# Half of the rotary sum moves from GpSimd to VectorE: the queries' 256 columns, behind the maximum

## The chip, the cores and the metric

The kernel runs on one core of one Trainium2 chip. The metric is the device time of one execution, in microseconds. A core has five engines that run their own instruction streams and meet at semaphores: TensorE (PE; PEld is its weight load), VectorE (DVE), ScalarE (ACT), GpSimd (POOL) and SyncE (SP, which issues the DMAs here).

## What is computed

The program is a decoder block on 32 sequences of 128 tokens and 128 channels: a causal self-attention, a cross-attention, and then a stack of six layers with windowed attention and a gated MLP. The change lies in the windowed attention of the six layers:

```
def attn_layer(x, Wqkv, qs, ksc, Wo):
    q, k, v = jnp.split(x @ Wqkv, 3, -1)            # 16 heads of 64
    q = l2norm(q) * qs
    k = l2norm(k) * ksc
    q = q * cos * scale + rotate_half(q) * sin * scale
    k = k * cos * inv   + rotate_half(k) * sin * inv
    out = local_attention(q, k, v)                  # window 32, looks one window back
    return out @ Wo
...
for i in range(6):
    x = attn_layer(shift_tokens(x), ...) + x
    x = ffn_layer(shift_tokens(x), ...) + x
```

The sum in the two lines of `q` and `k` is the rotary sum that this case is about.

## The kernel before

Everything stays in SBUF. Each of the six layers has 32 sequences times 4 groups of 4 heads, so 128 groups. One step of a software pipeline takes in one new group and works on several older ones at the same time: at step j the group j is projected, rotated and squared, the group j-3 is transposed (`win_heads`), the group j-5 gets its scores and its maximum, j-6 its exponentials and the scaling by the row sum, j-7 the transposition of the probabilities and the sum over the values, j-8 the output projection. Eight steps (two sequences) are the body of a hardware loop; steps 0 to 4 of a layer are written out separately and lie between the MLP of the layer before (`first` and `finish_into`). 30 of the 768 groups are in such opening steps, 738 in the main part. The MLP of the layer follows, partly woven into the drain.

There is no scheduler: each engine's order is written by hand, in its own block of the program, and waits are semaphore counts. In the main part VectorE does in each step, in this order: `win_cos` (L1487, projection times cosine table, 128x512 from PSUM), `win_sin` (L1495, projection with swapped halves times sine table), the reciprocal of the row sums (L1527), `win_scale` (L1537, probabilities), `win_max` (L1519), `win_norms` (L1502, sums of squares), `win_clamp` (L1512, small), and in some steps `win_tok` (L1463), `win_split` (L1469) and `win_add` (L1544), each of 128x128 and once in four steps. The latter three always stand in an odd step.

GpSimd does in each step `win_rotate` (L1206: `rotated = by_cos + by_sin`, 512 columns, 256 of the queries and 256 of the keys, all in SBUF), in each odd step `win_rnorm` (L1214: the power -1/2 of the 16 norms of two groups), and in each even step `win_unit` (L1226: two products of `rotated` by the norm's inverse). `win_unit` hands the group to TensorE's transposition (L691) by the semaphore `c_unit`. `win_cos` waits on the semaphore of `win_rotate` of two groups before (`c_rotated`), since the buffers `by_cos` and `by_sin` are two deep; `rotated` is four deep and comes free when TensorE has transposed the group (`c_heads`).

ScalarE does in each step the four exponentials of a group (L1052), the copy of the transposed probabilities (L1069), the squares (L1043), the copy of values and sums (L1063) and the copy of the transposed queries and keys (L1034). TensorE has in each step the projection (L698), the transposed probabilities (L757), band and scores (L730, L741), the value sum (L771), the transposition of heads (L691) and the output projection (L793).

Of the kernel before, what the change touches and what calls it, by code (L numbers as in the profile page):

```python
# [17 lines left out]
ALU = mybir.AluOpType  # L18
# [8 lines left out]
GROUPS = NB * NG  # L27
# [18 lines left out]
STEPS = 2 * NG  # L46
# [90 lines left out]
def has(index):  # L137

    return not isinstance(index, int) or index >= 0


def in_range(it, j, lag, n):

    return not isinstance(it, int) or 0 <= it * n[1] + j - lag < n[0]


def build(nc, x_in, ctx_in, a_w, a_m, b_wq, b_bq, b_wk, b_bk, b_wv, b_bv, b_wo, b_bo, wqkv, q_scale, k_scale,
          wo, ln_g, ln_b, w1, b1, w2, b2, const_d, out):
    with ExitStack() as stack:
# [3 lines left out]
        def ring(name, n, shape, dt=F32):  # L153
            return [sb(f"{name}{i}", shape, dt) for i in range(n)]
# [54 lines left out]
        by_cos = ring("by_cos", 2, [P, 2, HG, DH])  # L209
        by_sin = ring("by_sin", 2, [P, 2, HG, DH])  # L210
# [3 lines left out]
        rotated = ring("rotated", 4, [P, 2, HG, DH])  # L214
# [53 lines left out]
        def sem(name):  # L268
            return stack.enter_context(nc.semaphore(name))
# [90 lines left out]
        c_sin = sem("c_sin_done")  # L360
# [2 lines left out]
        c_nrm2 = sem("c_norm2")  # L363
        c_nrm2g = sem("c_norm2_guarded")
        c_rn = sem("c_rnorm")
        c_rot = sem("c_rotated")
        c_unit = sem("c_unit")
        c_heads = sem("c_heads")
        c_qk = sem("c_qk_ready")
# [71 lines left out]
        def here(it, j, lag):  # L441
            return in_range(it, j, lag, (GROUPS, STEPS))
# [720 lines left out]
        def _(pool):  # L1163
# [35 lines left out]
            def win_rotate(layer, it, j):  # L1199
                if here(it, j, 0):  # L1200
                    g = layer * GROUPS + it * STEPS + j
                    pool.wait_ge(c_sin, g + 1)
                    if has(it * STEPS + j - 4):

                        pool.wait_ge(c_heads, g - 3)
                    nc.gpsimd.tensor_tensor(rotated[j % 4][:, :, :, :], by_cos[j % 2][:, :, :, :], by_sin[j % 2][:, :, :, :], ALU.add).then_inc(c_rot, 1)  # L1206

            def win_rnorm(layer, it, j):
                if j % 2 == 1 and here(it, j, 1):
# [7 lines left out]
            def win_unit(layer, it, j):  # L1217
                if j % 2 == 0 and here(it, j, 2):
                    g = layer * GROUPS + it * STEPS + j - 2
                    u = layer * UNITS + it * (STEPS // 2) + j // 2 - 1  # L1220
                    slot = (j // 2 - 1) % 2
                    pool.wait_ge(c_rn, u + 1)
                    pool.wait_ge(c_rot, g + 2)
                    for i in range(2):
                        at = rotated[(j - 2) % 4 + i][:, :, :, :].rearrange("t a h d -> t (a h) d")
                        nc.gpsimd.tensor_tensor(at, at, rnorm[slot][:, i, :].unsqueeze(2).to_broadcast([P, 2 * HG, DH]), ALU.mult).then_inc(c_unit, 1)  # L1226

            def win_step(layer, it, j):
                win_rotate(layer, it, j)
                win_rnorm(layer, it, j)  # L1230
                win_unit(layer, it, j)
# [97 lines left out]
        def _(dve):  # L1329
# [141 lines left out]
            def win_tok_next(layer, it, j):  # L1471
                if j % NG == 1 and here(it, j, -2 * NG + 1):
                    win_tok(layer, it * 2 + j // NG + 2, j // NG)

            def win_split_next(layer, it, j):
                if j % NG == 3 and here(it, j, -2 * NG + 3):
                    win_split(layer, it * 2 + j // NG + 2, j // NG)

            def win_cos(layer, it, j):
                if here(it, j, 0):  # L1480
                    g = layer * GROUPS + it * STEPS + j
                    if has(it * STEPS + j - 2):

                        dve.wait_ge(c_rot, g - 1)
                    dve.wait_ge(c_proj, g + 1)
                    got = proj_ps[:, :].rearrange("t (a h d) -> t a h d", a=2, h=HG)
                    nc.vector.tensor_tensor(by_cos[j % 2][:, :, :, :], got, table(rot_cos, layer).unsqueeze(2).to_broadcast([P, 2, HG, DH]), ALU.mult).then_inc(c_cos, 1)  # L1487

            def win_sin(layer, it, j):
                if here(it, j, 0):  # L1490
                    if isinstance(it, int) and it == 0 and j == 0:
                        dve.wait_ge(c_sines, 2 * (layer + 1))
                    got = proj_ps[:, :].rearrange("t (n s d) -> t n s d", s=2, d=HALF)[:, :, ::-1, :]
                    rows = lambda b: b[:, :, :, :].rearrange("t a h (s d) -> t (a h) s d", s=2)
                    nc.vector.tensor_tensor(rows(by_sin[j % 2]), got, rows(sin_now), ALU.mult).then_inc(c_sin, 1)  # L1495

            def win_norms(layer, it, j):
                if here(it, j, 0):
                    g = layer * GROUPS + it * STEPS + j
                    dve.wait_ge(c_sq, g + 1)  # L1500
                    pair = norm2[j % 2]
                    nc.vector.tensor_reduce(pair[:, :, 0:1], squares[:, :, :], AX_X, ALU.add).then_inc(c_nrm2, 1)  # L1502

            def win_clamp(layer, it, j):
                if here(it, j, 0):
                    g = layer * GROUPS + it * STEPS + j
                    pair = norm2[j % 2]
                    dve.wait_ge(c_nrm2, g + 1)
                    if j % 2 == 0 and has(it * STEPS + j - 4):

                        dve.wait_ge(c_rn, layer * UNITS + it * (STEPS // 2) + j // 2 - 1)
                    nc.vector.tensor_reduce(norm2g[j // 2 % 2][:, j % 2, :].unsqueeze(2), pair[:, :, :], AX_X, ALU.max).then_inc(c_nrm2g, 1)  # L1512

            def win_max(layer, it, j):
                if here(it, j, WIN.top):
                    m = layer * GROUPS + it * STEPS + j - WIN.top
                    slot = (j - WIN.top) % 2
                    dve.wait_ge(c_scores, m + 1)
                    nc.vector.tensor_reduce(top[slot][:, :].rearrange("q (e i) -> q e i", e=2), win_ps[slot].rearrange("q e (i k) -> q e i k", i=2),  # L1519
                                            AX_X, ALU.max, negate=True).then_inc(c_top, 1)  # L1520

            def win_recip(layer, it, j):
                if here(it, j, WIN.scale):
                    m = layer * GROUPS + it * STEPS + j - WIN.scale
                    jl = (j - WIN.scale) % STEPS
                    dve.wait_ge(c_exp, m + 1)
                    nc.vector.reciprocal(rsum[jl % 2][:, :], psum_raw[jl % 2][:, :]).then_inc(c_rsum, 1)  # L1527

            def win_scale(layer, it, j):
                if here(it, j, WIN.scale):  # L1530
                    m = layer * GROUPS + it * STEPS + j - WIN.scale
                    jl = (j - WIN.scale) % STEPS
                    dve.wait_ge(c_rsum, m + 1)
                    if has(it * STEPS + j - WIN.scale - 2):

                        dve.wait_ge(c_pturn, m - 1)
                    nc.vector.tensor_tensor(prob[jl % 2][:, :, :].rearrange("q (e i) k -> q e i k", e=2), win_ps[jl % 2].rearrange("q e (i k) -> q e i k", i=2),  # L1537
                                            rsum[jl % 2][:, :].rearrange("q (e i) -> q e i", e=2).unsqueeze(3).to_broadcast([P, 2, 2, P]), ALU.mult).then_inc(c_scaled, 1)

            def win_add(layer, it, j):  # L1540
                if j % NG == 3 and here(it, j, WIN.out + NG - 1):
                    b = it * 2 + (j - WIN.out - NG + 1) // NG
                    dve.wait_ge(c_wo, layer * NB + b + 1)
                    nc.vector.tensor_tensor(seq(y, b), seq(y, b), acc_ps[:, 0:P], ALU.add).then_inc(c_yadd, 1)  # L1544

            def win_step(layer, it, j):
                win_cos(layer, it, j)
                win_sin(layer, it, j)
                win_recip(layer, it, j)
                win_scale(layer, it, j)  # L1550
                win_max(layer, it, j)
                win_norms(layer, it, j)
                win_clamp(layer, it, j)
                win_tok_next(layer, it, j)
                win_split_next(layer, it, j)
                win_add(layer, it, j)
# [93 lines left out]
            def win_rotations(layer, j):  # L1650
                win_cos(layer, 0, j)
                win_sin(layer, 0, j)

            def win_squares(layer, j):
                win_norms(layer, 0, j)
                win_clamp(layer, 0, j)
# [124 lines left out]
```

## Time and profile before

| | |
|---|---|
| device time, median of 3 runs | 4208.51 us (4206.87 to 4213.31) |
| the profiled execution | 4210.7 us, of which its span is 4208.9 us |
| TensorE busy | 3918.9 us (93%) |
| VectorE busy | 3703.7 us (88%) |
| ScalarE busy | 3550.0 us (84%) |
| GpSimd busy | 3379.4 us (80%) |

A line of the groups view names the line of the program, the engine, the operation, output and inputs, the count, then the busy time with the mean of one instruction, then the time for which the engine idled just before these instructions and what ended that idle time. Instructions of one engine overlap a little: the recorded duration of one is longer than the distance to the start of the next. A timeline row gives start and duration in microseconds. In the views over a part of the span, a window is given in microseconds from the start of the span.

### The profile page before, as it was taken

The page shows a single profiled execution, that of the slowest core. Times are in us where ns is not written, and L with a number is a line of the kernel's source. Part 1 is how long each engine was busy: PE and PEld are TensorE (multiplying, and loading weights), DVE is VectorE, ACT ScalarE, POOL GpSimd, SP SyncE. Part 2 cuts the span into 40 slices and gives each one's busy share as a digit, 9 for nine tenths or more (in the row PEclk, how much of TensorE's full clock was granted, in tenths as well). Part 3 has the DMA queues.
Part 4 walks back from the last instruction along what each step waited for, and adds up shares of the span by engine and source line. Part 5 has one row for each costly group of instructions (what it writes and reads, how often), then busy time and mean ns, then how long its engine had stood idle before and what let it go on. Part 6 is the DMA issues. An engine that isn't in the chain of part 4 may idle for free.

```text
span 4208.9 us, 137255 instructions
## 1 busy us (share of the span) xinstructions
PE 3918.9 (93%) x49504; PEld 3102.0 (74%) x49504; DVE 3703.7 (88%) x8896; ACT 3550.0 (84%) x11595; POOL 3379.4 (80%) x2461
## 2 busy tenths in 40 slices
PE   7998885999999999989999999999899999999998
PEld 5666664777777777777777777777777777777776
DVE  7998887999988999979999889999799998899996
ACT  6888995999977999959999779999599997699995
POOL 4554446999978999969999789999599997799993
PEclk9999997999999999999999999999999999999999
DMA  3000000000000000010000000000100000000001
GB/s 84 0 0 1 0 0 16 3 2 0 0 21 22 5 0 0 1 41 4 2 0 0 15 28 5 0 0 1 41 4 2 0 0 13 15 5 0 0 1 36
DMA packets 81122, 38.89 MB, mean 9 GB/s; under 512 B 60084, under 2 KB 73266, under 8 KB 80946
## 3 DMA queue, kind: packets, MB, share of 16 engines
q1 hardware_dynamic: 80946, 36.56, 3.3%
q8 instruction: 108, 1.77, 0.2%
q14 instruction: 68, 0.56, 0.0%
HBM read 21.92 MB, written 2.10 MB: 6 GB/s over the span
## 4 chain that ended last, share of the span: by engine, by line
ACT 42%; PE 33%; DVE 13%; issue 10%; POOL 2%; ACTq 1%; SPq 0%; DMA 0%; DVEq 0%; POOLq 0%
ACT pair L1052 20%; PE bank L771 12%; ACT prob_t L1069 7%; ACT vout L1063 6%; ACT qk_t L1034 5%; PE bank L691 5%; PE pair L848 4%; PE bank L698 3%; DVE top L1443 3%; PE bank L793 2%; DVE qk_parts L1418 2%; PE bank L864 2%; PE bank L672 1%; DVE by_sin L1411 1%; ACT prob L977 1%
## 5 line engine op out<-in xcount | busy, mean ns | idle before, releaser
L1214 POOL TENSOR_TENSOR rnorm<-norm2g,neg_half 128x16 f32<-128x16 f32 x384 | 1115.3, 2905 | 181.7 <-DVE norm2g L1512 172.4
L1052 ACT ACTIVATE pair<-pair,top 128x128 f32<-128x128 f32 x3072 | 1055.8, 345 | 34.9 <-DVE top L1519 24.2
L1206 POOL TENSOR_TENSOR rotated<-by_cos,by_sin 128x512 f32<-128x512 f32 x768 | 985.8, 1284 | 51.0 <-DVE by_sin L1495 44.4
L1226 POOL TENSOR_TENSOR rotated<-rotated,rnorm 128x512 f32<-128x512 f32 x768 | 785.3, 1043 | 0.5
L698 PE MATMUL bank<-wqkv_high,xt_high 128*128 128x512 f32 (+1 forms) x1536 | 649.5, 423 | 15.9 <-ACT squares L1043 14.5
L1052 ACT ACTIVATION_READ_ACCUMULATOR pair<-pair,top 128x1 f32 x3072 | 652.3, 212 | 0.0
L1487 DVE TENSOR_TENSOR by_cos<-bank,rot_cos 128x512 f32<-128x512 f32 x768 | 529.9, 690 | 108.2 <-PE bank L698 91.5
L1063 ACT ACTIVATE vout<-bank 128x512 f32<-128x512 f32 (+1 forms) x810 | 466.0, 575 | 150.5 <-PE bank L771 145.1
L771 PE MATMUL bank<-prob_t,vout 128*32 128x128 f32 x12288 | 495.2, 279 | 94.0 <-ACT prob_t L1069 56.8
L1537 DVE TENSOR_TENSOR prob<-pair,rsum 128x512 f32<-128x512 f32 x768 | 530.9, 691 | 40.0
L1043 ACT ACTIVATE squares<-bank 128x512 f32<-128x512 f32 x768 | 458.8, 597 | 109.7 <-DVE by_sin L1495 92.0
L1502 DVE TENSOR_REDUCE norm<-squares 128x8 f32<-128x512 f32 x768 | 519.3, 676 | 11.3 <-ACT squares L1043 9.9
L1519 DVE TENSOR_REDUCE top<-pair 128x4 f32<-128x512 f32 x768 | 522.4, 680 | 0.7
L1495 DVE TENSOR_TENSOR by_sin<-bank,sin_now 128x512 f32<-128x512 f32 x768 | 522.4, 680 | 0.0
L698 PE MATMUL bank<-wqkv_low,xt_high 128*128 128x512 f32 (+1 forms) x1536 | 520.6, 339 | 0.0
L698 PE MATMUL bank<-wqkv_high,xt_low 128*128 128x512 f32 (+1 forms) x1536 | 520.1, 339 | 0.0
L1196 POOL TENSOR_TENSOR kz_parts<-qk_parts,cst 128x512 fp32r<-128x512 f32 x256 | 266.2, 1040 | 307.4 <-DVE qk_parts L1418 307.4
L691 PE MATMUL bank<-cst,rotated 128*128 128x128 f32 x3072 | 504.3, 287 | 2.7 <-POOL rotated L1226 2.5
L1069 ACT ACTIVATE prob_t<-bank 128x512 f32<-128x512 f32 x768 | 474.3, 618 | 4.8 <-PE bank L757 4.8
L793 PE MATMUL bank<-wo_sb,vout 128*128 128x128 f32 x3072 | 472.8, 276 | 2.0 <-ACT vout L1063 2.0
L771 PEld LDWEIGHTS bank<-prob_t,vout 128*32 128x32 f32 x12288 | 289.8, 109 | 239.6 <-ACT prob_t L1069 196.5
L757 PE MATMUL bank<-cst,prob 128*128 128x128 f32 x3072 | 461.8, 273 | 1.4 <-ACT qk_t L1034 1.4
(142 smaller groups left out, 8451.6 us busy)
## 6 DMA issues: line engine op xcount, KB each, us to landing
wqkv_sb<-in_L_ffn_Wqkv_dram SPq DMA_DIRECT2D x36, 256.0 KB, 4.0
ctx_all<-y SPq DMA_DIRECT2D x48, 128.0 KB
ctx_all<-y SPq DMA_DIRECT2D x48, 127.0 KB
wo_sb<-in_L_ffn_Wo_dram SPq DMA_DIRECT2D x48, 64.0 KB, 2.0
out_dram<-y SPq DMA_DIRECT2D x8, 256.0 KB, 3.5
w_sb<-in_L_ffn_W_dram SPq DMA_DIRECT2D x6, 341.0 KB, 3.0
w_sb<-in_L_ffn_W_dram SPq DMA_DIRECT2D x12, 64.0 KB
cst<-in_constants_dram SPq DMA_DIRECT2D x1, 582.0 KB, 3.9
```

The source lines that it names most:

```text
L691: last = nc.tensor.transpose(turned_ps(it)[:, k * P:(k + 1) * P], flat[:, k * P:(k + 1) * P], ident)
L698: last = nc.tensor.matmul(dst, a[slot][:, :], w[:, which, cols], start=(n == 0), stop=(n == 2))
L771: last = nc.tensor.matmul(value_ps[PAD * h:PAD * (h + 1), half * P:(half + 1) * P], vout[jl][:, at:at + PAD], prob_t[jl % 2][:, h % 2 * 2 ...
L793: last = nc.tensor.matmul(acc_ps[:, 0:P], vout[(j - 1) % STEPS][:, half * P:(half + 1) * P], wo_sb[:, k * P:(k + 1) * P], start=(k == 0), ...
L1052: last = nc.scalar.activation(at, at, ACT.Exp, bias=top[jl % 2][:, h:h + 1], accum_out=psum_raw[jl % 2][:, h:h + 1])
L1063: nc.scalar.activation(vout[j][:, cols], value_ps[:, cols], ACT.Copy).then_inc(c_vout, 1)
L1069: nc.scalar.activation(prob_t[(j - WIN.probs) % 2][:, :, :].rearrange("k h q -> k (h q)"), turn_c_ps[:, :], ACT.Copy).then_inc(c_pt, 1)
L1206: nc.gpsimd.tensor_tensor(rotated[j % 4][:, :, :, :], by_cos[j % 2][:, :, :, :], by_sin[j % 2][:, :, :, :], ALU.add).then_inc(c_rot, 1)
L1214: nc.gpsimd.tensor_tensor(rnorm[slot][:, :, :].rearrange("t g n -> t (g n)"), norm2g[slot][:, :, :].rearrange("t g n -> t (g n)"), neg_hal ...
L1226: nc.gpsimd.tensor_tensor(at, at, rnorm[slot][:, i, :].unsqueeze(2).to_broadcast([P, 2 * HG, DH]), ALU.mult).then_inc(c_unit, 1)
L1487: nc.vector.tensor_tensor(by_cos[j % 2][:, :, :, :], got, table(rot_cos, layer).unsqueeze(2).to_broadcast([P, 2, HG, DH]), ALU.mult).then_ ...
L1537: nc.vector.tensor_tensor(prob[jl % 2][:, :, :].rearrange("q (e i) k -> q e i k", e=2), win_ps[jl % 2].rearrange("q e (i k) -> q e i k", i=2),
```

## The change

The queries' half (index 0 of the second axis, 256 columns) of the sum `by_cos + by_sin` is done by a new VectorE instruction, behind the maximum of the same step; GpSimd keeps the keys' half. The semaphore of the sum becomes two, `c_keys_rotated` and `c_queries_rotated`. The new instruction waits for VectorE's own product with the sine table and for the buffer; GpSimd's `win_unit` waits for both halves. In the opening steps the new instruction stands right behind the sine product.

```
-                    nc.gpsimd.tensor_tensor(rotated[j % 4][:, :, :, :], by_cos[j % 2][:, :, :, :], by_sin[j % 2][:, :, :, :], ALU.add).then_inc(c_rot, 1)
+                    nc.gpsimd.tensor_tensor(rotated[j % 4][:, 1, :, :], by_cos[j % 2][:, 1, :, :], by_sin[j % 2][:, 1, :, :], ALU.add).then_inc(c_rot, 1)
...
                     pool.wait_ge(c_rn, u + 1)
                     pool.wait_ge(c_rot, g + 2)
+                    pool.wait_ge(c_qrot, g + 2)
...
+            def win_rotate_queries(layer, it, j):
+                if here(it, j, 0):
+                    g = layer * GROUPS + it * STEPS + j
+                    dve.wait_ge(c_sin, g + 1)
+                    if has(it * STEPS + j - 4):
+
+                        dve.wait_ge(c_heads, g - 3)
+                    nc.vector.tensor_tensor(rotated[j % 4][:, 0, :, :], by_cos[j % 2][:, 0, :, :], by_sin[j % 2][:, 0, :, :], ALU.add).then_inc(c_qrot, 1)
...
                 win_max(layer, it, j)
+                win_rotate_queries(layer, it, j)
                 win_norms(layer, it, j)
...
             def win_rotations(layer, j):
                 win_cos(layer, 0, j)
                 win_sin(layer, 0, j)
+                win_rotate_queries(layer, 0, j)
```

VectorE, an odd step of the loop in the main part, before (output <- inputs, then what the instruction waits for):

```order
710 L1487 TENSOR_TENSOR by_cos<-bank,rot_cos 128x512 [waits c_proj]
711 L1495 TENSOR_TENSOR by_sin<-bank,sin_now 128x512
712 L1527 RECIPROCAL rsum<-psum_raw 128x4 [waits c_exp]
713 L1536 REGISTER_ALU [waits c_rsum]
714 L1537 TENSOR_TENSOR prob<-pair,rsum 128x512 [waits c_pturn]
715 L1518 REGISTER_ALU
716 L1519 TENSOR_REDUCE top<-pair 128x4 [waits c_scores]
717 L1502 TENSOR_REDUCE norm<-squares 128x8 [waits c_squares_done]
718 L1512 TENSOR_REDUCE norm2g<-norm 128x8 [waits c_norm2]
```

The same step of VectorE now:

```order
728 L1489 TENSOR_TENSOR by_cos<-bank,rot_cos 128x512 [waits c_proj]
729 L1497 TENSOR_TENSOR by_sin<-bank,sin_now 128x512
730 L1538 RECIPROCAL rsum<-psum_raw 128x4 [waits c_exp]
731 L1547 REGISTER_ALU [waits c_rsum]
732 L1548 TENSOR_TENSOR prob<-pair,rsum 128x512 [waits c_pturn]
733 L1530 TENSOR_REDUCE top<-pair 128x4 [waits c_scores]
734 L1505 REGISTER_ALU [waits c_sin_done]
735 L1506 TENSOR_TENSOR rotated<-by_cos,by_sin 128x256 [waits c_heads]
736 L1513 TENSOR_REDUCE norm<-squares 128x8 [waits c_squares_done]
737 L1523 TENSOR_REDUCE norm2g<-norm 128x8 [waits c_norm2]
```

One instruction with two SBUF inputs and its register work are new between maximum and norms; nothing else on VectorE changes place.

GpSimd, an even and an odd step of the same loop, before:

```order
293 L1206 TENSOR_TENSOR rotated<-by_cos,by_sin 128x512 [waits c_heads]
294 L1222 REGISTER_ALU
295 L1226 TENSOR_TENSOR rotated<-rotated,rnorm 128x512 [waits c_rotated,c_rnorm]
296 L1226 TENSOR_TENSOR rotated<-rotated,rnorm 128x512
297 L1202 REGISTER_ALU
298 L1206 TENSOR_TENSOR rotated<-by_cos,by_sin 128x512 [waits c_heads,c_sin_done]
299 L1214 TENSOR_TENSOR rnorm<-norm2g,neg_half 128x16 [waits c_norm2_guarded]
```

The same of GpSimd now:

```order
293 L1207 TENSOR_TENSOR rotated<-by_cos,by_sin 128x256 [waits c_heads]
294 L1223 REGISTER_ALU
295 L1228 TENSOR_TENSOR rotated<-rotated,rnorm 128x512 [waits c_queries_rotated,c_keys_rotated,c_rnorm]
296 L1228 TENSOR_TENSOR rotated<-rotated,rnorm 128x512
297 L1203 REGISTER_ALU
298 L1207 TENSOR_TENSOR rotated<-by_cos,by_sin 128x256 [waits c_heads,c_sin_done]
299 L1215 TENSOR_TENSOR rnorm<-norm2g,neg_half 128x16 [waits c_norm2_guarded]
```

GpSimd's order stays; its sum is half as wide and the first product waits for one semaphore more.

## Rows read from the trace of the kernel before

**Rows 1.** The page: the chain that ended last, by engine and by line.
```profile
ACT 42%; PE 33%; DVE 13%; issue 10%; POOL 2%; ACTq 1%; SPq 0%; DMA 0%; DVEq 0%; POOLq 0%
ACT pair L1052 20%; PE bank L771 12%; ACT prob_t L1069 7%; ACT vout L1063 6%; ACT qk_t L1034 5%; PE bank L691 5%; PE pair L848 4%; PE bank L698 3%; DVE top L1443 3%; PE bank L793 2%; DVE qk_parts L1418 2%; PE bank L864 2%; PE bank L672 1%; DVE by_sin L1411 1%; ACT prob L977 1%
```

**Rows 2.** Busy time by stretch: length, busy us (count) by engine, clock, DMA.
```profile
750.00:1150.00 400.00, 391.85 (x5564) 313.36 (x5561) 364.48 (x784) 368.92 (x1238) 374.26 (x255) 1.00 0.01 2
```

**Rows 3.** Groups of VectorE in the stretch 750 to 1150 us.
```profile
L1487 DVE TENSOR_TENSOR by_cos<-bank,rot_cos 128x512 f32<-128x512 f32 x101 | 69.7, 690 | 14.7 <-PE bank L698 11.6
...
L1469 DVE TENSOR_TENSOR xt_low<-bank,xt_high 128x128 fp32r<-128x128 f32 x25 | 7.3, 292 | 7.2 <-ACT xt_high L1023 7.2
L1463 DVE TENSOR_REDUCE tok<-y 128x128 f32 x25 | 7.2, 286 | 1.0
```

**Rows 4.** Groups of GpSimd in the same stretch.
```profile
L1214 POOL TENSOR_TENSOR rnorm<-norm2g,neg_half 128x16 f32<-128x16 f32 x51 | 148.2, 2905 | 25.6 <-DVE norm2g L1512 24.2
L1206 POOL TENSOR_TENSOR rotated<-by_cos,by_sin 128x512 f32<-128x512 f32 x102 | 130.4, 1278 | 0.9
L1226 POOL TENSOR_TENSOR rotated<-rotated,rnorm 128x512 f32<-128x512 f32 x102 | 104.4, 1045 | 0.0
```

**Rows 5.** ScalarE's waits in the same stretch: us in total, times, longest.
```profile
ACT vout L1063 <- PE bank L771: 22.6, 102, 0.3
```

**Rows 6.** Timeline of VectorE and GpSimd, loop steps with `tok`, then with `xt_low`.
```profile
905.60 0.17 DVE L1512 TENSOR_REDUCE norm2g<-norm 128x8 f32<-128x16 f32 x1
905.72 0.29 DVE L1463 TENSOR_REDUCE tok<-y 128x128 f32 x1
...
908.68 0.68 DVE L1502 TENSOR_REDUCE norm<-squares 128x8 f32<-128x512 f32 x1
...
908.72 1.28 POOL L1206 TENSOR_TENSOR rotated<-by_cos,by_sin 128x512 f32<-128x512 f32 x1
...
913.21 0.17 DVE L1512 TENSOR_REDUCE norm2g<-norm 128x8 f32<-128x16 f32 x1
...
914.41 0.69 DVE L1487 TENSOR_TENSOR by_cos<-bank,rot_cos 128x512 f32<-128x512 f32 x1 [0.26 <-PE bank L698]
...
916.32 1.27 POOL L1206 TENSOR_TENSOR rotated<-by_cos,by_sin 128x512 f32<-128x512 f32 x1
917.12 0.68 DVE L1502 TENSOR_REDUCE norm<-squares 128x8 f32<-128x512 f32 x1
917.55 2.05 POOL L1226 TENSOR_TENSOR rotated<-rotated,rnorm 128x512 f32<-128x512 f32 x2
```

**Rows 7.** Timeline of VectorE early in the first layer, where no wait is named.
```profile
717.29 0.69 DVE L1487 TENSOR_TENSOR by_cos<-bank,rot_cos 128x512 f32<-128x512 f32 x1
...
720.62 0.17 DVE L1512 TENSOR_REDUCE norm2g<-norm 128x8 f32<-128x16 f32 x1
720.70 0.68 DVE L1487 TENSOR_TENSOR by_cos<-bank,rot_cos 128x512 f32<-128x512 f32 x1
```

**Rows 8.** Single lines: duration ns min/median/max, first and last start, forms.
```profile
L1374 DVE TENSOR_TENSOR x<-x,b_o x32: 274/278/286, 337.9 to 636.8; 128x128 f32 x26, 128x128 f32<-128x128 f32 x6
...
L1570 DVE TENSOR_TENSOR y<-y,b_sb x48: 675/679/691, 1240.7 to 4198.3; 128x512 f32 x24, 128x512 f32<-128x512 f32 x24
...
L1294 POOL TENSOR_TENSOR sin_now<-cst,qk_scale x12: 717/720/724, 688.2 to 3545.7; 128x256 f32<-128x256 f32 x12
```

**Rows 9.** Timeline of VectorE and GpSimd where they meet at SBUF operands.
```profile
714.07 0.23 DVE L1669 TENSOR_SCALAR mlp_now<-per_layer 128x8 f32<-128x8 f32 x1
...
1283.64 2.91 POOL L1214 TENSOR_TENSOR rnorm<-norm2g,neg_half 128x16 f32<-128x16 f32 x1 [1.82 <-DVE norm2g L1512]
1284.33 0.68 DVE L1570 TENSOR_TENSOR y<-y,b_sb 128x512 f32<-128x512 f32 x1
...
2460.89 0.68 DVE L1570 TENSOR_TENSOR y<-y,b_sb 128x512 f32<-128x512 f32 x1
2461.05 1.66 POOL L1206 TENSOR_TENSOR rotated<-by_cos,by_sin 128x512 f32<-128x512 f32 x1
2462.67 2.04 POOL L1226 TENSOR_TENSOR rotated<-rotated,rnorm 128x512 f32<-128x512 f32 x2
2462.78 0.96 DVE L1669 TENSOR_SCALAR mlp_now<-per_layer 128x8 f32<-128x8 f32 x1
```

More of the change, by code:

```diff
@@ L365, in build @@
         c_rn = sem("c_rnorm")
-        c_rot = sem("c_rotated")
+        c_rot = sem("c_keys_rotated")
+        c_qrot = sem("c_queries_rotated")
         c_unit = sem("c_unit")
```

## The prediction, made blind

> **What bounds the kernel now.** I read the chain that ended last first. It runs over ScalarE for 42% and over TensorE for 33%, and GpSimd, which the change relieves, is on it for 2%, or 84 of 4208.9 us [rows 1]. The reader is to see there that a shorter GpSimd has little to give back. Then the busy time of a stretch in the main part, 750 to 1150 us: of 400 us TensorE is busy for 391.9, GpSimd for 374.3, ScalarE for 368.9 and VectorE for 364.5, at full clock [rows 2]. All four are nearly full, so the question is which of them has real slack. The groups tell: `by_cos` occurs 101 times in the 400 us, so a step takes 400 / 101 = 3.960 us [rows 3]. ScalarE waits only for the value sum, 22.6 us in 102 waits, 0.22 us a step [rows 5], and that wait is part of its ring with TensorE (exponentials, transposed probabilities, value sum, copy). This ring sets the pace. VectorE waits 14.7 us at `by_cos` for TensorE's projection, 7.2 us at `xt_low` for ScalarE, and 1.0 us at `tok`: 22.9 / 101 = 0.227 us a step [rows 3]. GpSimd waits 25.6 us, a quarter of a microsecond a step, nearly all of it for VectorE's norms [rows 4]; it follows VectorE.
>
> **What the change removes.** GpSimd's sum falls from 1278 ns [rows 4] to about the 720 ns of its one two-input instruction with 256 columns [rows 8]: 0.56 us less in every step. Nothing on the chain waits for it: before, GpSimd idles for VectorE already, and what it saves becomes more of that idle time. I count this as 0. Its bounds are 0 and the 84 us of its share of the chain.
>
> **What the change adds.** A sum of 128x256 on VectorE with both inputs in SBUF. The trace has no such row, but it has both neighbours: 278 ns for 128x128 and 679 ns for 128x512 [rows 8]. Between them 401 ns for 384 columns; for 256 columns that gives 278 + 128 x 401 / 384 = 412 ns. What counts is the distance to the next start. Full-width instructions stand 0.08 us closer than they last (`norm2g` at 720.62 lasts 0.17 and its successor starts at 720.70 [rows 7]), so 0.333 us. The ends are 0.33 and 0.41; I take 0.333, since the next instruction, the norms, waits for squares that were there before.
>
> How much of it hides? VectorE's step without its waits is 3.960 - 0.227 = 3.733 us. This may still hold unnamed waiting: in the loop the successor of `norm2g` starts 0.12 us behind it at best [rows 6], where the unrolled steps have 0.08 [rows 7], and `norm2g` counts with its full 0.17 in my subtraction. So up to 0.09 us may come off; I take half, 0.045. VectorE's step becomes 3.733 - 0.045 + 0.333 = 4.021 us, above the ring's 3.960. The cover is the 0.227 us (0.27 with the unnamed part), the new work is 0.333, and from there on VectorE is the pace. Queued behind the new instruction are the norms and `norm2g`, for which GpSimd's `rnorm` waits, and the next step's cosine and sine products, for which the squares on ScalarE wait. With VectorE setting the pace, its waits for the projection and for `xt_high` close up, for those engines then run ahead of it.
>
> **The shared operand path.** Both inputs of the new instruction are in SBUF, and so are GpSimd's. In the trace such pairs hold each other up. GpSimd's sum of 1278 ns takes 1.66 us when it starts 0.16 us behind VectorE's two-input `y` sum; a 128x8 `mlp_now` that takes 0.23 us alone takes 0.96 when GpSimd's product had started 0.11 us before it, and it ends 1.07 us behind the product's start, as the product's half of 2.04 us ends. But the `y` sum at 1284.33 takes its normal 0.68 although `rnorm` runs over all of it [rows 9]. So a GpSimd sum or product that was first holds VectorE until about 0.2 us before its own end (2462.67 to 2462.78 + 0.96 - 0.23 = 2463.51, 0.84 of 1.02), and `rnorm` doesn't.
> The Trainium skill says the same in "SBUF — State Buffer" (Who interferes with whom): a VectorE instruction with two SBUF inputs and a GpSimd instruction that reads SBUF exclude each other, and the second one blocks until the first finishes. The trace agrees for sums and products with the 1.66 and 0.96 us; for `rnorm` the trace's 0.68 us speaks against "any GpSimd instruction that reads", and the measured row decides.
>
> Where does the new instruction fall? In an odd step GpSimd ends its two products, does its short sum and waits for the norms; the new slot, 1.4 us behind the sine product's end, is free. In an even step GpSimd comes out of `rnorm` and starts its sum 3.12 us behind the last `norm2g` (905.60 to 908.72; 913.21 to 916.32 gives 3.11). After a step with `tok` the new slot is today's start of the norms, 3.08 us behind that `norm2g` (908.68), a little less without waits: VectorE comes first, GpSimd waits 0.3 us, which it has. After a step with `xt_low` the slot is at 3.91 us (917.12) with 0.6 us or so of waits in it; without them it is at 3.3, inside GpSimd's short sum, which holds until 3.12 + 0.72 - 0.2 = 3.64 [rows 6, 8]. So about 0.38 us once in four steps, 0.095 a step. Its ends are 0 and the full product, priced below as a rival.
>
> **The sum.** Per step 4.021 + 0.095 - 3.960 = 0.156 us; 738 steps of the main part make 115 us. In the 30 opening steps VectorE has idle time behind the sine product in the first layer and little of it in the others: 0.41 us x 25 x about a fifth, 2 us. Together 117 us on the profiled execution's 4210.7, or 4328 us; the median of the runs, 4208.5, is 2 us lower, which I leave out. Low end: 3.733 - 0.09 + 0.333 = 3.976, no blocking, 0.016 x 738 = 12 us, 4223. High end: no unnamed waiting, blocking as above, and half of the 0.227 us not closing up: 3.733 + 0.333 + 0.095 + 0.113 - 3.960 = 0.314 x 738 = 232 us, 4443.
>
> **The rivals.**
> The instruction costs its length only (VectorE sets the pace, but first at SBUF in every step): 0.061 x 738 + 2 = 47 us, 4258. For it: in odd steps and behind `tok` the slot is free. Against it: the slot behind `xt_low`.
> The blocking is the larger term: in even steps the new instruction comes when one of GpSimd's two products has started and waits up to 0.84 us. If this meets the even steps behind `xt_low`, it adds 0.84 x 185 = 155 us in place of the 70 of my 0.095: 4413; in all 369 even steps, with half of 0.84 in the others, 78 more, 4491. For it: the slot lies within 0.5 us of the products' start. Against it: the shorter sum and the closed waits put the slot ahead of them. The Trainium skill's rule in the section named above, taken whole, would add `rnorm` to what blocks; in even steps only its last 0.1 us could be met.
> Not slower: VectorE's step hides the new work entirely. Its place is the end of VectorE's step: early in the first layer a step without `tok` takes 720.70 - 717.29 = 3.41 us [rows 7]. Were the loop's steps the same, 3.41 + 0.17 for the small instructions (25 each of `tok`, `xt_low` and their like at 0.2 us, over four steps) + 0.333 = 3.91 would stay under 3.960, the ring would stay the pace, and the time would be 4211, or some us less if GpSimd's earlier products let TensorE transpose earlier. It decides at a free time of 0.333 us a step. For it: those rows. Against it: the loop has register work that the unrolled rows lack, and GpSimd's 2% of the chain; and any blocking breaks it.
> That the change doesn't do what it says, I don't see: the order of both engines has it.
>
> **How the numbers follow.** Forecast 0.55; bare length 0.15; larger blocking 0.15; hidden 0.10; a loss of less than 30 us, between hidden and forecast, 0.05. A difference of 0.2%, 8.4 us, is about what a measurement can tell here. Hidden splits into 0.06 same and 0.04 faster; all else is slower, 0.90. The range of 4240 to 4440 holds the forecast, the bare length and the milder half of the larger blocking, and leaves out the hidden case and 4491.
>
> **What would show it.** In the profile of the changed kernel the step of the stretch 750 to 1150 us should be near 4.12 us, so 97 instances of `by_cos`; VectorE's named waits near zero; the new instruction at 412 ns as its shortest, with a second cluster of longer ones, once in four steps, 0.3 to 0.4 us more; the chain should run over VectorE; GpSimd's busy time should fall by some 0.56 x 768 = 430 us and its wait for `norm2g` grow; ScalarE should wait for the maximum or the sine product. I am wrong if the idle time at `by_cos` is still there (the ring still sets the pace), if the new instruction's mean is above 0.7 us (blocking by the products), or if GpSimd has become later rather than earlier.

## The result, and the profile after

The changed kernel takes 4341.1 us (median of 4 runs, 4340.0 to 4342.9) against 4208.9 us before: 1.031 times as long, with an interval of 1.030 to 1.033. The prediction said 4328 us, 4240 to 4440.

The chain that ended last, on the page of the changed kernel, by engine and by line. It ran over ScalarE and TensorE before [rows 1].

```profile
DVE 58%; issue 19%; PE 10%; ACT 9%; DVEq 1%; POOL 1%; SPq 0%; DMA 0%; ACTq 0%; POOLq 0%
DVE top L1530 11%; DVE by_sin L1497 10%; DVE norm L1513 9%; DVE by_cos L1489 7%; DVE rotated L1506 7%; PE pair L849 4%; DVE top L1445 3%; ACT pair L1053 2%; DVE qk_parts L1420 2%; DVE rsum L1538 1%; PE bank L865 1%; PE bank L772 1%; DVE by_sin L1413 1%; ACT vout L1064 1%; ACT prob L978 1%
```

VectorE has taken the chain over. Line numbers are shifted: L1489 is `by_cos`, L1506 the new sum, L1207 GpSimd's sum of the keys. The same stretch as in [rows 2], busy us by engine (PE, PEld, DVE, ACT, POOL), then clock and DMA:

```profile
750.00:1150.00 400.00, 381.15 (x5324) 296.14 (x5323) 383.09 (x845) 344.12 (x1182) 312.62 (x241) 1.00 0.01 2
```

VectorE's busy time rose from 364.5 to 383.1 of 400 us and all the others fell. The groups of VectorE in that stretch, which answer to [rows 3]:

```profile
L1489 DVE TENSOR_TENSOR by_cos<-bank,rot_cos 128x512 f32<-128x512 f32 x97 | 66.7, 688 | 4.0 <-issue 3.4
...
L1506 DVE TENSOR_TENSOR rotated<-by_cos,by_sin 128x256 f32<-128x256 f32 x96 | 48.7, 507 | 0.0
...
L1471 DVE TENSOR_TENSOR xt_low<-bank,xt_high 128x128 fp32r<-128x128 f32 x24 | 7.0, 292 | 0.0
```

97 instances of `by_cos` instead of 101. The waiting before `by_cos` fell from 14.7 to 4.0 us and no longer ends with a result of TensorE (the 3.4 us called "issue" come once per turn of the eight-step loop, 12 times in the stretch), and the 7.2 us before `xt_low` are gone, as a pace-setting engine should have it. Where they went, in the waits of the same stretch (us in total, times, longest):

```profile
POOL rnorm L1215 <- DVE norm2g L1523: 78.7, 49, 1.8
ACT squares L1044 <- DVE by_sin L1497: 48.9, 95, 1.0
```

Before, ScalarE waited in this stretch for the value sum [rows 5] and, which rows 5 leave out, for one transposition:

```profile
ACT xt_high L1023 <- PE bank L673: 5.7, 25, 0.2
```

Now it waits half a microsecond a step for the sine product, and GpSimd waits three times as long for the norms as in [rows 4].

The new sum alone, over all its instances: duration in ns min/median/max.

```profile
L1506 DVE TENSOR_TENSOR rotated<-by_cos,by_sin x768: 414/416/1008, 698.6 to 4244.0; 128x256 f32<-128x256 f32 x192
```

The shortest is 414 ns (412 was estimated), and the mean in the stretch is 507, so 0.093 us a step is holding: time by which the recorded duration exceeds the unheld one because a GpSimd instruction came first. The timeline of VectorE and GpSimd (start us, duration us) shows where:

```profile
902.23 0.41 DVE L1506 TENSOR_TENSOR rotated<-by_cos,by_sin 128x256 f32<-128x256 f32 x1
902.30 0.93 POOL L1207 TENSOR_TENSOR rotated<-by_cos,by_sin 128x256 f32<-128x256 f32 x1
...
905.98 0.41 DVE L1506 TENSOR_TENSOR rotated<-by_cos,by_sin 128x256 f32<-128x256 f32 x1
...
910.14 0.74 POOL L1207 TENSOR_TENSOR rotated<-by_cos,by_sin 128x256 f32<-128x256 f32 x1
910.18 0.98 DVE L1506 TENSOR_TENSOR rotated<-by_cos,by_sin 128x256 f32<-128x256 f32 x1
...
914.62 0.41 DVE L1506 TENSOR_TENSOR rotated<-by_cos,by_sin 128x256 f32<-128x256 f32 x1
...
927.08 0.56 DVE L1506 TENSOR_TENSOR rotated<-by_cos,by_sin 128x256 f32<-128x256 f32 x1
```

At 902.23 VectorE comes first and GpSimd's sum takes 0.93 instead of 0.73; at 910.18 GpSimd came 0.04 us earlier and VectorE takes 0.98. Both 910.18 and 927.08 are even steps behind a step with `xt_low`: two in eight are held, by 0.57 and 0.15 us. The chain in order of time has this long instance again and again, always 33.17 us apart (start, us):

```profile
910.27 0.89 DVE rotated L1506
...
943.44 0.90 DVE rotated L1506
```

Eight steps in 33.17 us are 4.146 us a step, 4.146 - 0.093 = 4.053 without holding, against 3.960 before.

### The profile page after: what moved, and what is told of

Its sections match the earlier page's. It is cut to its first block, busy times and chain, and to the rows that moved or that the text cites. A ratio compares the mean times of both kernels' runs of the same rounds, so it can differ in the third digit from the quotient of the medians.

```text
span 4340.3 us, 138676 instructions
## 1 busy us (share of the span) xinstructions
PE 3970.8 (91%) x49504; PEld 3081.9 (71%) x49504; DVE 3983.1 (92%) x9664; ACT 3482.8 (80%) x11595; POOL 3025.2 (70%) x2461
## 4 chain that ended last, share of the span: by engine, by line
DVE 58%; issue 19%; PE 10%; ACT 9%; DVEq 1%; POOL 1%; SPq 0%; DMA 0%; ACTq 0%; POOLq 0%
DVE top L1530 11%; DVE by_sin L1497 10%; DVE norm L1513 9%; DVE by_cos L1489 7%; DVE rotated L1506 7%; PE pair L849 4%; DVE top L1445 3%; ACT pair L1053 2%; DVE qk_parts L1420 2%; DVE rsum L1538 1%; PE bank L865 1%; PE bank L772 1%; DVE by_sin L1413 1%; ACT vout L1064 1%; ACT prob L978 1%
## 5 line engine op out<-in xcount | busy, mean ns | idle before, releaser
L1228 POOL TENSOR_TENSOR rotated<-rotated,rnorm 128x512 f32<-128x512 f32 x768 | 814.4, 1079 | 0.5
L1207 POOL TENSOR_TENSOR rotated<-by_cos,by_sin 128x256 f32<-128x256 f32 x768 | 596.7, 777 | 110.4 <-DVE by_sin L1497 110.4
L1053 ACT ACTIVATION_READ_ACCUMULATOR pair<-pair,top 128x1 f32 x3072 | 673.3, 219 | 0.0
L1489 DVE TENSOR_TENSOR by_cos<-bank,rot_cos 128x512 f32<-128x512 f32 x768 | 527.9, 687 | 28.8 <-issue 20.8
L758 PE MATMUL bank<-cst,prob 128*128 128x128 f32 x3072 | 477.1, 278 | 3.0 <-ACT qk_t L1035 1.4
L758 PEld LDWEIGHTS bank<-cst,prob 128*128 128x128 f32 x3072 | 353.2, 141 | 173.1 <-ACT qk_t L1035 85.7
```

What stands on the lines that cost most here:

```text
L758: last = nc.tensor.transpose(turn_c_ps[:, h * P:(h + 1) * P], prob[jl % 2][:, h, :], ident)
L1053: last = nc.scalar.activation(at, at, ACT.Exp, bias=top[jl % 2][:, h:h + 1], accum_out=psum_raw[jl % 2][:, h:h + 1])
L1207: nc.gpsimd.tensor_tensor(rotated[j % 4][:, 1, :, :], by_cos[j % 2][:, 1, :, :], by_sin[j % 2][:, 1, :, :], ALU.add).then_inc(c_rot, 1)
```

## The experiments

The theory from here on is called A: VectorE sets the pace, and its price is the new instruction's length plus the time for which a GpSimd sum or product that started first holds it. B: only the length costs. C, which the expectations name once: what costs is how late GpSimd and TensorE get their input. Every edit is against the changed kernel, except in the second. Medians of the runs; the kernel before ran beside them with 4212.1 us in the first four and 4208.4 us in the others.

**One SBUF input instead of two.**

```
-nc.vector.tensor_tensor(rotated[j % 4][:, 0, :, :], by_cos[j % 2][:, 0, :, :], by_sin[j % 2][:, 0, :, :], ALU.add)
+nc.vector.tensor_reduce(flat(rotated[j % 4])[:, 0:256], flat(by_cos[j % 2])[:, 0:256].unsqueeze(2), AX_X, ALU.add)
```

(`flat` stands here and below for the view of a buffer with its 512 columns in one axis.)

> The new VectorE instruction stays in its place with its 256 columns and its waits, but reads by_cos alone (a reduction over an axis of length 1, which copies); the queries' sine part is left out of the computation. Same length (about 0.42 us), only one SBUF input. Theory A: no instance is longer than 0.43 us, the step falls from 4.147 to 4.054 us, 4341 - 69 = 4272. Theory B: the same 4341, and the long instances were idle time that shows elsewhere. Either way GpSimd's sums lose their longer instances (0.93, 0.81 us).

Measured: 4277.5 us, 1.016 times before (1.014 to 1.017). The sum's group in the stretch, and its single line over all instances:

```profile
L1506 DVE TENSOR_REDUCE rotated<-by_cos 128x256 f32<-128x256 f32 x99 | 40.6, 410 | 0.0
```

```profile
L1506 DVE TENSOR_REDUCE rotated<-by_cos x768: 403/409/422, 698.0 to 4177.4; 128x256 f32<-128x256 f32 x192
```

None of 768 is longer than 0.422 us. It has the same place, columns and waits and nearly the same length, so the 64 us between 4341 and 4277 go with the second SBUF input, as A had it. (The operation changed too, from TENSOR_TENSOR to TENSOR_REDUCE; the timelines, in which every long instance meets a GpSimd sum, speak for the input.) What stays over the kernel before, some 65 to 69 us, is what the length costs beyond the free time that VectorE had.

**GpSimd's relief alone** (against the kernel before).

```
-nc.gpsimd.tensor_tensor(rotated[j % 4][:, :, :, :], by_cos[j % 2][:, :, :, :], by_sin[j % 2][:, :, :, :], ALU.add)
+nc.gpsimd.tensor_tensor(rotated[j % 4][:, 1, :, :], by_cos[j % 2][:, 1, :, :], by_sin[j % 2][:, 1, :, :], ALU.add)
```

(Nobody writes the queries' half in the steps; GpSimd sets it to zero once, ahead of everything.)

> The kernel before, with GpSimd summing the keys' 256 columns only; nobody sums the queries' half, which is left out of the computation. It is the change's relief of GpSimd by itself. Theory A: GpSimd only follows, so 4209 within 8 us, although its busy time falls by 430 us. A rival in which GpSimd's lateness costs something: up to 84 us less, 4125.

Measured: 4207.1 us, 0.999 times before (0.998 to 1.000). Busy time on its page:

```profile
PE 3915.1 (93%) x49504; PEld 3099.7 (74%) x49504; DVE 3702.9 (88%) x8896; ACT 3552.4 (84%) x11595; POOL 2966.3 (71%) x2465
```

GpSimd lost 413 us of work, and the kernel gained about 5 us.

**The sum before the maximum**, 0.6 us earlier.

```
                 win_scale(layer, it, j)
+                win_rotate_queries(layer, it, j)
                 win_max(layer, it, j)
-                win_rotate_queries(layer, it, j)
```

> The new VectorE sum stands before the maximum instead of behind it, 0.6 us earlier in every step; nothing else changes. Theory A (VectorE sets the pace, and once in four steps the sum is held by a GpSimd sum that had started, 0.093 us a step): the even slots leave GpSimd's sum, which takes 0.093 x 738 = 69 us off, 4272; but in half of the odd steps the earlier slot falls into GpSimd's sum at 905.19 (slot 905.39), some 0.2 us once in four steps, which gives 37 us back: 4272 to 4310. Theory B (only the instruction's length costs; the long instances are harmless): 4341, no change. Theory C (what costs is what GpSimd and TensorE wait for): 4341 or more, since the order against them hardly changes.

Measured: 4321.9 us, 1.026 times before (1.024 to 1.028), a little above A's upper end of 4310 and clear of B's 4341. The timeline, odd steps:

```profile
903.73 0.73 POOL L1207 TENSOR_TENSOR rotated<-by_cos,by_sin 128x256 f32<-128x256 f32 x1
904.11 0.62 DVE L1506 TENSOR_TENSOR rotated<-by_cos,by_sin 128x256 f32<-128x256 f32 x1
```

The even steps are free, and the odd ones have become the place of the holding, as expected; the mean holding fell from 93 to 471 - 415 = 56 ns. C had expected 4341 or more, so it is out.

**GpSimd keeps all 512 columns and VectorE does the queries as well**, into a buffer of its own.

```
-nc.gpsimd.tensor_tensor(rotated[j % 4][:, 1, :, :], by_cos[j % 2][:, 1, :, :], by_sin[j % 2][:, 1, :, :], ALU.add)
+nc.gpsimd.tensor_tensor(rotated[j % 4][:, :, :, :], by_cos[j % 2][:, :, :, :], by_sin[j % 2][:, :, :, :], ALU.add)
...
-nc.vector.tensor_tensor(rotated[j % 4][:, 0, :, :], ...)
+nc.vector.tensor_tensor(spare[:, :, :], ...)
```

> GpSimd keeps the whole sum of 512 columns as before, and VectorE does the queries' sum as well, in the changed kernel's place, into a buffer that nobody reads. Theory A: the length alone would give 4272, but GpSimd's sum now holds VectorE for up to 1.1 us where it is met, in the even steps behind xt_low and now in odd steps too, where GpSimd's work ends later: 4400 to 4550. Theory B (length only): 4341 as the changed kernel, or 4272.

Measured: 4603.6 us, 1.093 times before (1.091 to 1.095), above the range given for A and far from B. The sum in the stretch, then two places in the timeline:

```profile
L1507 DVE TENSOR_TENSOR spare<-by_cos,by_sin 128x256 f32<-128x256 f32 x89 | 76.9, 864 | 0.0
```

```profile
903.05 1.27 POOL L1208 TENSOR_TENSOR rotated<-by_cos,by_sin 128x512 f32<-128x512 f32 x1
903.39 1.21 DVE L1507 TENSOR_TENSOR spare<-by_cos,by_sin 128x256 f32<-128x256 f32 x1
...
908.35 1.28 POOL L1208 TENSOR_TENSOR rotated<-by_cos,by_sin 128x512 f32<-128x512 f32 x1
908.80 1.11 DVE L1507 TENSOR_TENSOR spare<-by_cos,by_sin 128x256 f32<-128x256 f32 x1
```

The same instruction now lasts 864 ns on average, and half of its instances are held. So GpSimd's halved sum did have a use in the changed kernel: it kept the holding small.

**The sum behind the norms**, 0.6 us later.

```
                 win_norms(layer, it, j)
+                win_rotate_queries(layer, it, j)
                 win_clamp(layer, it, j)
```

> The new VectorE sum stands behind the norms, 0.6 us later than in the changed kernel. Two effects are expected apart. Length: norm2g waits 0.71 us from the start of the norms for their result, of which 0.6 is the norms' own place; the sum fills this gap, so VectorE's unblocked step falls from 4.054 by 0.11 to 3.94 us, just under the 3.960 of ScalarE and TensorE. Theory A (held by GpSimd's sum or product that started first): in even steps behind xt_low the slot now comes about 3.86 us behind the last norm2g, when GpSimd's first product (from 3.82) has begun, and is held some 0.8 us, 0.2 a step: 4.14 us a step, 4320 to 4350. Theory B (length only): 4209 to 4220.

Measured: 4220.3 us, 1.003 times before (1.002 to 1.004). A's number missed by 100 us. The number is B's, but the mechanism isn't, for the instances are held more than in the changed kernel (547 ns on average against 507). The sum in the stretch:

```profile
L1506 DVE TENSOR_TENSOR rotated<-by_cos,by_sin 128x256 f32<-128x256 f32 x101 | 55.2, 547 | 0.0
```

The timeline of VectorE, one odd step, where nothing is held:

```profile
905.61 0.68 DVE L1513 TENSOR_REDUCE norm<-squares 128x8 f32<-128x512 f32 x1
906.20 0.42 DVE L1506 TENSOR_TENSOR rotated<-by_cos,by_sin 128x256 f32<-128x256 f32 x1
906.53 0.16 DVE L1523 TENSOR_REDUCE norm2g<-norm 128x8 f32<-128x16 f32 x1
906.61 0.27 DVE L1465 TENSOR_REDUCE tok<-y 128x128 f32 x1
```

And the same place of the changed kernel:

```profile
922.47 0.41 DVE L1506 TENSOR_TENSOR rotated<-by_cos,by_sin 128x256 f32<-128x256 f32 x1
922.80 0.68 DVE L1513 TENSOR_REDUCE norm<-squares 128x8 f32<-128x512 f32 x1
923.51 0.17 DVE L1523 TENSOR_REDUCE norm2g<-norm 128x8 f32<-128x16 f32 x1
923.61 0.29 DVE L1471 TENSOR_TENSOR xt_low<-bank,xt_high 128x128 fp32r<-128x128 f32 x1
```

The held instances stand in the even steps. Two of them, the first behind GpSimd's sum, the second behind the first of its two products:

```profile
909.65 0.74 POOL L1207 TENSOR_TENSOR rotated<-by_cos,by_sin 128x256 f32<-128x256 f32 x1
910.00 0.67 DVE L1506 TENSOR_TENSOR rotated<-by_cos,by_sin 128x256 f32<-128x256 f32 x1
...
917.99 1.04 POOL L1228 TENSOR_TENSOR rotated<-rotated,rnorm 128x512 f32<-128x512 f32 x1
918.43 0.88 DVE L1506 TENSOR_TENSOR rotated<-by_cos,by_sin 128x256 f32<-128x256 f32 x1
```

547 - 414 = 133 ns of holding a step, where I had expected 0.2 us: the products were met once in eight steps and not once in four, for 0.47 us and not 0.8, and the other even steps met GpSimd's sum, for 0.26 us at most. The larger error is the length: I counted 0.11 us for the filled gap. From the norms to `norm2g` are 0.92 us here, with the sum between them, and the next instruction starts 0.08 us behind, 1.00 us in all; in the changed kernel the same stretch (sum, norms at 922.80, `norm2g` at 923.51, next at 923.61) takes 0.33 + 0.71 + 0.10 = 1.14 us, and in three of eight steps norms to `norm2g` take 0.80 instead of 0.71 (911.08 to 911.88). Averaged over the steps of the stretch, the distances behind sum, norms and `norm2g` add up, without the holding, to 1.02 us here and 1.22 us there, so the filled gap is worth 0.20 us.

The step is 3.968 us (31.74 us from one start of `by_cos` to the eighth behind it). Of it 0.133 is holding and 0.037 is waiting that the groups view names (3.7 us in 101 steps), so VectorE's unheld step is 3.80 us and not 3.94. Even with the holding it stays under 3.960, and VectorE no longer sets the pace alone. The chain on the page is shared:

```profile
DVE 32%; ACT 28%; PE 25%; issue 12%; DVEq 1%; POOL 1%; SPq 0%; ACTq 0%; DMA 0%; POOLq 0%
```

**128 columns on VectorE, 384 on GpSimd.** 

```
-nc.vector.tensor_tensor(rotated[j % 4][:, 0, :, :], by_cos[j % 2][:, 0, :, :], by_sin[j % 2][:, 0, :, :], ALU.add)
+nc.vector.tensor_tensor(flat(rotated[j % 4])[:, 0:128], flat(by_cos[j % 2])[:, 0:128], flat(by_sin[j % 2])[:, 0:128], ALU.add)
...
-nc.gpsimd.tensor_tensor(rotated[j % 4][:, 1, :, :], by_cos[j % 2][:, 1, :, :], by_sin[j % 2][:, 1, :, :], ALU.add)
+nc.gpsimd.tensor_tensor(flat(rotated[j % 4])[:, 128:512], flat(by_cos[j % 2])[:, 128:512], flat(by_sin[j % 2])[:, 128:512], ALU.add)
```

> VectorE sums only the first 128 of the queries' columns, GpSimd the other 384. VectorE's length falls by 0.133 us a step: unblocked 3.92 us, under the 3.960 of the other two. Theory A: GpSimd's sum now takes about 1.0 us and holds VectorE until 3.9 us behind the last norm2g, so the even slots behind xt_low lose 0.4 us and odd slots may lose too: 0.1 to 0.16 a step, of which 0.04 is free: 4255 to 4300. Theory B (length only): 4209, no change against before.

Measured: 4352.1 us, 1.034 times before (1.032 to 1.036). VectorE does half as many columns as in the changed kernel, and the time is 11 us longer. The sum in the stretch, then GpSimd's:

```profile
L1506 DVE TENSOR_TENSOR rotated<-by_cos,by_sin 128x128 f32<-128x128 f32 x96 | 50.5, 526 | 0.0
```

```profile
L1207 POOL TENSOR_TENSOR rotated<-by_cos,by_sin 128x384 f32<-128x384 f32 x96 | 97.3, 1013 | 9.9 <-DVE by_sin L1497 9.9
```

An instruction that takes 279 ns at its shortest takes 526 on average: GpSimd's longer sum of 1.01 us holds it in half of the steps, 0.247 us a step. B's 4209 is out; A's direction held, but its 0.1 to 0.16 us was too little.

**All 512 columns on VectorE.** 

```
-                    pool.wait_ge(c_rot, g + 2)
...
             def win_step(layer, it, j):
-                win_rotate(layer, it, j)
...
-                        dve.wait_ge(c_rot, g - 1)
+                        dve.wait_ge(c_qrot, g - 1)
...
-nc.vector.tensor_tensor(rotated[j % 4][:, 0, :, :], by_cos[j % 2][:, 0, :, :], by_sin[j % 2][:, 0, :, :], ALU.add)
+nc.vector.tensor_tensor(flat(rotated[j % 4])[:, 0:512], flat(by_cos[j % 2])[:, 0:512], flat(by_sin[j % 2])[:, 0:512], ALU.add)
```

> VectorE sums all 512 columns in the changed kernel's place and GpSimd none. Length 0.6 instead of 0.333 us: unblocked 4.054 + 0.267 = 4.32 us a step. Theory B (length only): 4209 + 0.36 x 738 = 4475. Theory A: GpSimd has no sum left, but starts its two products as soon as rnorm ends, 3.1 us behind the last norm2g; the even slots behind xt_low (3.3 us) are held until about 3.96, 0.7 us once in four steps, 0.175 a step: 4604.

Measured: 4526.1 us, 1.075 times before (1.074 to 1.077), between B and A. The sum in the stretch:

```profile
L1504 DVE TENSOR_TENSOR rotated<-by_cos,by_sin 128x512 f32<-128x512 f32 x92 | 69.8, 759 | 0.0
```

The products hold it, but only for 759 - 675 = 84 ns a step on average, not for 175. The timeline shows why: behind one `xt_low` the products are first, behind the next VectorE is, by 0.07 us.

```profile
902.61 2.49 POOL L1227 TENSOR_TENSOR rotated<-rotated,rnorm 128x512 f32<-128x512 f32 x2 [0.16 <-POOL rnorm L1215]
902.87 1.33 DVE L1504 TENSOR_TENSOR rotated<-by_cos,by_sin 128x512 f32<-128x512 f32 x1
...
920.71 0.68 DVE L1504 TENSOR_TENSOR rotated<-by_cos,by_sin 128x512 f32<-128x512 f32 x1
920.78 1.51 POOL L1227 TENSOR_TENSOR rotated<-rotated,rnorm 128x512 f32<-128x512 f32 x1
```

So the size of one holding, 1.33 - 0.68 = 0.65 us, is near the 0.7 us expected, and it comes once in eight steps instead of once in four. (The chain on this run's page names GpSimd with 29% and "issue" with 49%. But in the stretch GpSimd waits 154.1 of 400 us for VectorE's norms, while VectorE's only named wait is 3.5 us, so VectorE sets the pace here too.)

**Two places, by the step's parity.**

```
                 win_recip(layer, it, j)
+                if j % 2 == 0:
+                    win_rotate_queries(layer, it, j)
                 win_scale(layer, it, j)
                 win_max(layer, it, j)
-                win_rotate_queries(layer, it, j)
                 win_norms(layer, it, j)
+                if j % 2 == 1:
+                    win_rotate_queries(layer, it, j)
```

> The changed kernel with the new sum in two places by the step's parity: in even steps between the reciprocal and the scaling, where rnorm (which holds nobody) runs on GpSimd; in odd steps between the norms and norm2g, where GpSimd is idle. Both places also fill a wait of VectorE for its own result (about 0.1 us each). Theory A: no instance longer than 0.43 us, unblocked step 4.054 less about 0.1 = 3.95 us, so ScalarE and TensorE set the pace again: 4205 to 4235. Theory B (only length, without the gaps): 4277. It gains nothing over the kernel before, since GpSimd's relief is worth 0.1% at most.

Measured: 4215.4 us, 1.002 times before (1.001 to 1.003). Single line, then the timeline of an even step:

```profile
L1506 DVE TENSOR_TENSOR rotated<-by_cos,by_sin x768: 408/424/427, 696.6 to 4119.2; 128x256 f32<-128x256 f32 x192
```

```profile
898.78 2.90 POOL L1215 TENSOR_TENSOR rnorm<-norm2g,neg_half 128x16 f32<-128x16 f32 x1 [1.17 <-DVE norm2g L1523]
900.67 0.42 DVE L1506 TENSOR_TENSOR rotated<-by_cos,by_sin 128x256 f32<-128x256 f32 x1
901.65 0.73 POOL L1207 TENSOR_TENSOR rotated<-by_cos,by_sin 128x256 f32<-128x256 f32 x1
```

None of 768 instances is held, although the sum at 900.67 lies wholly inside `rnorm`. This kernel and the one with the sum behind the norms give the loss back to within 0.3%. Neither beats the kernel before, which fits the 2% that GpSimd had on the chain and the 5 us that its relief was worth alone.

**The runs together.** Take the unheld 4277.5 us of the one-input run as the base, add what the columns change in VectorE's length (0.60 us of distance for 512, 0.333 for 256, 0.20 for 128) and the mean holding, times 738 steps:

| kernel | length, us a step | holding, us a step | worked out | measured |
|---|---|---|---|---|
| changed | 0 | 0.093 | 4346 | 4341 |
| before the maximum | 0 | 0.056 | 4319 | 4322 |
| extra sum | 0 | 0.449 | 4609 | 4604 |
| 128 columns | -0.133 | 0.247 | 4362 | 4352 |
| 512 columns | +0.267 | 0.084 | 4537 | 4526 |

Five kernels with times 280 us apart follow from two terms to within 11 us. The two kernels with the sum in a wait of VectorE are left out, since there VectorE doesn't set the pace alone. The holding is read from the traces afterwards, so the table shows that the two terms account for the times, not that they could be forecast; the forecasts of the holding were off in size in four of the runs (behind the norms, extra sum, 128 and 512 columns).

## Why the prediction was right

**The pace.** The step was to pass from the ring of ScalarE and TensorE to VectorE. It did: the chain is 58% VectorE, its named waits in the stretch fell to 3.4 us, ScalarE waits for the sine product. (That ScalarE waited only for the value sum before leaves out 5.7 us at `xt_high`; no term hangs on it.)

**The cover and the length.** The cover was put at 0.227 us in named waits and 0.045 in unnamed ones, against 0.333 us of work; so 4.021 us without holding. Measured is 4.053, so the sum was 0.032 us a step or 24 us too low. The 0.045 is the term at fault; without it the sum gives 4.066, 0.013 too much. Unnamed waiting there was, but it stayed. `norm2g` in the stretch, before, after, and with the sum behind the norms:

```profile
L1512 DVE TENSOR_REDUCE norm2g<-norm 128x8 f32<-128x16 f32 x101 | 17.2, 170 | 6.9
```

```profile
L1523 DVE TENSOR_REDUCE norm2g<-norm 128x8 f32<-128x16 f32 x96 | 16.3, 170 | 6.6
```

```profile
L1523 DVE TENSOR_REDUCE norm2g<-norm 128x8 f32<-128x16 f32 x101 | 16.0, 159 | 0.0
```

It went only where another instruction was put into it.

**The holding.** It was put at 0.38 us once in four steps, 0.095 a step, in the even steps behind `xt_low`. Measured is 0.093, in those steps, as 0.57 and 0.15 by turns. The mean agrees better than the argument deserves: it was worked out from a slot at 3.3 us behind `norm2g`, and by turns the slot comes at 3.15 us (907.03 to 910.18) and at 3.57 us (923.51 to 927.08). The forecast's own figures, 3.64 - 3.3, also give 0.34 us and not 0.38. That the number came out is thus partly luck; that there is such a term, and that it goes with the second SBUF input, the one-input run shows.

**GpSimd's relief** was put at 0. Alone it is worth 5 us (interval 0.4 to 9 us), and its busy time fell by 354 us and not 430, mostly since GpSimd is held too: its sum takes 777 ns on average on the changed kernel's page against 736 for the half sum alone, and its products 1079 against 1047.

**The sum.** 0.156 us a step was forecast; 4.146 - 3.960 = 0.186 came in the stretch, which would be 137 us in 738 steps, against 132 measured. Over all six layers the starts of `by_cos` from step 5 to the last step span 3014.9 us against 2880.5, so 134 us came in the main part and nothing in the opening steps, where 2 us were expected.

**The rivals.** Bare length (4258) is what the one-input run shows, 4277, and so not the changed kernel. The larger holding (4413 to 4491) didn't come: in the stretch all held instances meet GpSimd's sum and none meets a product. How dear holding can be, the extra-sum run shows, though there it is GpSimd's sum of 1.28 us that holds: 4604. Hidden entirely (4211) failed on the loop: its unheld step is 4.053 us and not the 3.91 that the unrolled rows suggest. (The 0.17 us in that sum should have been 0.15, three instructions of 0.2 us in four steps, which doesn't change this.) It became nearly true in the last run, 4215, by other places for the same instruction.

## What to carry to other kernels

Work that is taken from an engine that only follows buys next to nothing (here 5 us for 413 us of work); ask what the receiving engine's free time per step is, in its named waits, and compare that with the start-to-start distance of the new instruction. A VectorE instruction with two SBUF inputs has a second price, set by what GpSimd does at its slot: in this kernel a place 0.6 us later, or two places by parity, took the time down by 3%, while half as many columns took nothing off. In this kernel the good places were beside `rnorm`, the small power instruction that held nobody, and behind an instruction for whose result the next one waits.

## What the runs showed that was not expected

- An instruction put into the wait for an own result costs less than its length: from the start of the norms to the start behind `norm2g` 1.00 us with a 0.33 us sum in between, against 0.81 (0.71 + 0.10) without it, so that the sum costs 0.19 there and not 0.33. The steps with 0.80 in place of 0.71 are absent where the gap is filled; what makes these steps longer, no run here shows.
- A GpSimd sum or product holds VectorE's two-input instruction until 0.13 us before its recorded end (910.14 + 0.74 against 910.18 + 0.98 - 0.41; behind a sum it is 0.12 to 0.14 us in every held instance between 760 and 1150 us of five kernels, with sums of 0.73 to 1.28 us), whereas `rnorm`, which reads 16 columns and takes 2.9 us, doesn't hold it at any point in which they met. The Trainium skill's "SBUF — State Buffer" (Who interferes with whom) calls the shared port pair an exclusive lock and has a VectorE instruction with two SBUF inputs contend with a GpSimd instruction that reads SBUF. The rows agree for the sums and products, and on issue order deciding who blocks; for `rnorm`, which reads SBUF too, none of the 768 sums of the last run, half of which are placed beside it, took more than 0.427 us, and the measurement decides.
- Halving the VectorE part (128 columns for 256) made the kernel slower (4352 against 4341): the GpSimd part grew, and with it the holding from 0.093 to 0.247 us a step.
